# TensorE's loop over the routed expert blocks written out, with fewer loads of expert numbers

## The reference

```
router_probs = softmax(x @ gate_w + gate_b)
values, indices = top_k(router_probs, k=2);  values /= sum(values) + 1e-9
h = gelu(x @ ew1[e] + eb1[e]);  all_outputs[e] = h @ ew2[e] + eb2[e]
moe_out = sum over the two chosen experts of value * all_outputs
return x + mlp_shared(x) + moe_out
```

## Time and profile before

| | |
|---|---|
| median of 3 runs | 920.14 us (920.0 to 920.22) |
| the profiled execution | 923.21 us, span 921.5 us |
| TensorE matmul busy | 686.9 us, 75% of the span |
| VectorE, ScalarE, GpSimd busy | 668.0, 520.6, 474.9 us |
| first routed stage | about 170 to 295 us |
| second routed stage | about 707 to 832 us |

### The profile page before, as it was taken

The page is one execution under the profiler, slowest core; times in us unless marked ns, Lnnn a source line. Parts: engine busy times, 40 slices in busy tenths (PEclk is TensorE's granted clock), DMA queues, the critical chain, the costliest instruction groups (busy, mean ns, idle before and its releaser), DMA issues.

```text
span 921.5 us, 23822 instructions
## 1 busy us (share of the span) xinstructions
PE 686.9 (75%) x7840; PEld 493.2 (54%) x7841; DVE 668.0 (72%) x1374; ACT 520.6 (56%) x1212; POOL 474.9 (52%) x459
## 2 busy tenths in 40 slices
PE   1365299699999258899899899992897999995000
PEld 1243299588889223344344444431896998885000
DVE  7889968477775348899899899967794777772222
ACT  3275454366666144888888888873643766662000
POOL 3974306678780778482340300002256888835775
PEclk9999589799999755999899999996797999998555
DMA  6230210133343111010000000000201233341223
GB/s 181 81 80 0 59 34 1 47 93 84 88 80 55 52 46 35 7 36 14 0 0 0 0 0 0 2 1 23 70 2 30 81 83 90 85 67 49 74 77 86
DMA packets 55995, 43.65 MB, mean 47 GB/s; under 512 B 8228, under 2 KB 50120, under 8 KB 55944
## 3 DMA queue, kind: packets, MB, share of 16 engines
q0 software_dynamic: 9088, 18.63, 9.5%
q1 hardware_dynamic: 46856, 24.35, 9.3%
HBM read 26.44 MB, written 16.52 MB: 47 GB/s over the span
## 4 chain that ended last, share of the span: by engine, by line
PE 47%; POOL 19%; DVE 17%; issue 9%; ACT 3%; DMA 3%; DVEq 1%; SPq 0%; POOLq 0%; ACTq 0%
PE ps L659 26%; POOL scratch L594 10%; POOL gy L608 8%; PE ps L770 6%; PE ps L966 6%; DVE xn L1352 5%; PE ps L785 4%; DVE mx L1656 2%; PE ps L979 2%; DVE hl L1359 1%; PE ps L676 1%; PE ps L824 1%; DMA scratch<-rows,tok_i 1%; DVE rnorm L1380 1%; DMA xres<-in_L_attn_a_x 1%
## 5 line engine op out<-in xcount | busy, mean ns | idle before, releaser
L594 POOL DMA_INDIRECT scratch<-rows,tok_i x156 | 183.2, 1175 | 53.5 <-issue 46.6
L1136 ACT ACTIVATE h<-ps,b1T 128x256 f32<-128x256 f32 x440 | 171.7, 478 | 62.3 <-PE ps L659 62.3
L1656 DVE TENSOR_REDUCE mx<-ps 128x2 f32<-128x512 f32 x256 | 171.3, 687 | 24.9 <-PE ps L659 23.2
L1240 ACT ACTIVATE scratch<-ps 128x512 f32<-128x512 f32 x256 | 148.1, 601 | 36.2 <-PE ps L659 34.7
L608 POOL DMA_INDIRECT gy<-ysorted,slot_i x128 | 122.0, 953 | 76.1 <-DMA ysorted<-yst 38.1
L659 PE MATMUL ps<-xg,w1s 128*128 128x256 f16 x936 | 119.6, 280 | 9.6 <-issue 9.4
L770 PE MATMUL ps<-w2s,hhi 128*128 x1248 | 117.3, 219 | 0.0
L659 PEld LDWEIGHTS ps<-xg,w1s 128*128 x936 | 89.8, 100 | 24.3 <-issue 13.1
L659 PE MATMUL ps<-kst,qst 32*128 32x256 f16 x512 | 93.3, 289 | 8.8 <-DVE mx L1656 8.6
L1505 DVE SCALAR_TENSOR_TENSOR hlo<-h,hhi 128x1024 f16<-128x1024 f32 x78 | 95.6, 1225 | 2.7
L1162 ACT ACTIVATE xg<-ps 128x512 f16<-128x512 f16 x78 | 46.6, 597 | 88.7 <-PE ps L824 88.7
(11 more groups left out here) (215 smaller groups left out, 1348.6 us busy)
## 6 DMA issues: line engine op xcount, KB each, us to landing
ysorted<-yst SPq DMA_DIRECT2D x78, 128.0 KB, 1.8
h<-in_L_ffn_ew SPq DMA_DIRECT2D x16, 256.0 KB, 3.1
rows<-hl SPq DMA_DIRECT2D x8, 512.0 KB, 3.5
scratch<-rows,tok_i POOLq DMA_INDIRECT x156
xres<-in_L_attn_a_x SPq DMA_DIRECT2D x4, 512.0 KB, 5.8
gy<-ysorted,slot_i POOLq DMA_INDIRECT x128, 2.5
out_x<-xres SPq DMA_DIRECT2D x4, 512.0 KB, 3.3
b2s<-in_L_ffn_eb SPq DMA_DIRECT2D x1, 512.0 KB, 4.9
```

Source lines behind the costliest of these rows:

```text
L594: pool.indirect_dma_start(grow[:, BT * (f % 4) + t, :], None, rows_dram[r], bass.IndirectOffsetOnAxis(ap=tok_i[:, n:n + 1], axis=0))\
L1136: last = act.activation(h32[:, u % 2, f], HB[u % 2][:, f], ACT.Gelu_apprx_tanh, bias=b1T[:, ds(e * CH + c, 1)], scale=1.0 / PS)
L1240: act.activation(prb[:, (s // 4 * 4 + (s + 2) % 4) % 8, :], ps[:, s % 2, :], ACT.Exp, scale=HD ** -0.5 / (PS * PS))\
L1656: dve.tensor_reduce(mx[:, c, j:j + 5:4], ps[:, 2 + s % 2, :].rearrange("p (n k) -> p n k", n=2), AX_X, ALU.max).then_inc(Att.mx, 1)
```

## The change

TensorE's hardware loop is replaced by the 39 iterations written out, in the same order of `up_routed`, `turn` and `down_routed`. The numbers of the experts are now loaded when they are first needed and kept in a table `ahead`. At the start 13 elements are loaded (0 to 12), ahead of n = 11 eleven (13 to 23), ahead of n = 22 eleven (24 to 34), and ahead of n = 33 four (35 to 38). That is 4 loads and 39 elements in a stage. Semaphores are compared with constants. Nothing changes on the other engines.

```
-                es = experts(0, 2)
-                up_routed(0, 0, es[0])
+                ahead = {n: e for n, e in enumerate(experts(0, 13))}
+                up_routed(0, 0, ahead[0])
                 turn(2, 2, 0)
-                up_routed(1, 1, es[1])
-                with pe.Fori(0, LOOPED) as i:
-                    es = experts(4 * i, 6)
-                    for u in range(4):
-                        n = 4 * i + u
-                        up_routed(n + 2, (u + 2) % 4, es[u + 2])
-                        turn(n + 3, (u + 3) % 4, i + (u + 3) // 4)
-                        down_routed(n, u, es[u])
-                es = experts(NBLK - 3, 3)
-                for u in range(3):
-                    if u < 1:
-                        up_routed(NBLK - 1, 2, es[2])
+                up_routed(1, 1, ahead[1])
+                for n in range(NBLK):
+                    if n + 2 < NBLK:
+                        if n + 2 not in ahead:
+                            more = experts(n + 2, min(11, NBLK - n - 2))
+                            ahead.update({n + 2 + j: e for j, e in enumerate(more)})
+                        up_routed(n + 2, (n + 2) % 4, ahead[n + 2])
                     else:
-                        up_shared(SA + u - 1)
-                    down_routed(NBLK - 3 + u, u, es[u])
+                        up_shared(SA + n + 2 - NBLK)
+                    if n + 3 < NBLK:
+                        turn(n + 3, (n + 3) % 4, (n + 3) // 4)
+                    down_routed(n, n % 4, ahead[n])
```

## The result

| | before | after |
|---|---|---|
| median of the timed runs | 921.7 us (918.53 to 924.43, 20 runs) | 917.84 us (913.68 to 922.48, 20 runs) |
| ratio | | 0.9958, 95% interval 0.9945 to 0.997 |
| profiled execution | span 921.5 us | span 915.8 us, run 917.55 us |

The change makes the kernel faster by 0.42%, interval 0.3 to 0.55%. On the 921.7 us that is 3.9 us, where 6.3 were forecast. 917.84 lies at the upper end of the range 912 to 918, but the gain is some 60% of the one forecast. Beside the runs of before taken with it the gain is that of rival 1 (920.14 - 916.4 = 3.7 us).

A forecast was written before the change was run, and what follows sets the result against it. TensorE was taken to bound the routed stages. Seams -11.74, loads +5.04 and gathers +0.4 gave -6.3 us, from a median of 920.14 to 913.8 us, range 912.0 to 918.0.

The forecast's parts named there:

- rival 1: Load of eleven from 13: an unaligned start makes all reads singles, 2.6 us more, 916.4 us; chance 0.24.
- The seams: TensorE's lost time between loop passes and at loop exits vanishes: 5.69 us in stage one, 6.05 in stage two, together 11.74.
- the 0.72 at the exit of stage two: Time TensorE lost where stage two leaves its loop, counted among the savings.
- The price of the load of eleven from 13: Load ahead of n = 11: taken as 3 + 2 reads, 0.75 us felt a stage; bound with all singles 2.05.
- head, 13 from 0: Load at a stage's start: three groups and a single, 1.13 us, fully felt, 0.58 over the load of before.
- The 0.57: Microseconds of each inner load expected to lie hidden behind matmuls already handed over, read at the exit of stage one.
- rival 3: Six inner loads: less of each lies hidden behind matmuls, 0.5 us more each, 916.8 us; chance 0.09.
- Instruction supply: Fetches for the longer written-out stream, some 24 to 32 in all, hidden by matmuls: cost 0.
- rival 5: Instruction fetches stop TensorE in the written-out code; at 0.65 us each 18.2 us, 932.0 us; chance 0.05.
- Rival 4: Every element is a read of its own, in long loads at least: slower by 2.8 us, 922.9 us; chance 0.07.
- The gathers: GpSimd's row fetches speed up with TensorE; 0.4 us added for late rows in stage two, between 0 and 1.3.
- Rival 2: Gathers keep their own pace: stage two gains only its exit, 0.72 us, stage one 3.2; 916.2 us; chance 0.09.

The follow-up runs named there:

- c2: Kernel before with its loop kept, but constants as expert numbers and no register loads on TensorE; ratio 1.0018 to the kernel before (922.3 us).
- e2: Kernel before with its loop written out, loads of 12, 12, 12 and 3 from multiples of four; ratios 0.9939 to 0.9966 on 989 us chips, 0.9898 on a 922 us chip.
- c1: Kernel before with its loop written out, constants as expert numbers and no register loads on TensorE; ratio 1.0024 to the kernel before (922.3 us).
- e6: Kernel before with its loop written out, ten loads of four from multiples of four; ratio 0.9919 on a 989 us chip, 0.9888 on a 922 us chip.
- e5: Kernel before with its loop kept, two loads of four from multiples of four in each pass instead of one of six; ratios 0.9945 and 0.9934.
- a1: The changed kernel run again, unaltered, on a 989 us chip; ratio 0.9986 to the kernel before (991.5 us).

## Why the prediction was wrong

**The seams: right.** All of them went, and nothing took their place at other blocks. The mechanism needs one correction. The branch with what surrounds it makes no seam alone (c2: steps of 2.87), and the load would cost little alone (in e2, loads of 0.96 to 1.09 us cost 0.25 to 0.37). It is their sum of 0.57 + 0.82 = 1.4 us that runs over the lead of 0.7 by 0.7. One seam was mis-sized: the 0.72 at the exit of stage two came behind a stop for rows, and in the two later traces of the kernel before that exit loses 0.3.

**The price of the load of eleven from 13: wrong, and this is the step that failed.** The prediction put it at 1.32 us of load and 0.75 felt, "since TensorE's six already mix groups and singles". It took 2.71 and 2.73 us and cost 2.03 and 2.01. The reason given was a reading of the wrong load: the six start at a multiple of four, and so say nothing of a load that doesn't. The one from 13 got no groups at all, though two aligned ones lie inside it. ScalarE's 916 ns for four from 4i + 2 couldn't decide either, since they hold no aligned group, so rival 1 was wrong to count it as support. The rows of before were silent, and the sum took the cheaper of two readings. The dearer adds 2.54 us, about the whole of the missing gain.

**The other terms**, predicted and measured in stages one and two:

| | predicted | measured |
|---|---|---|
| head, 13 from 0 | 0.58 | 0.60, 0.53 |
| n = 11 | 0.75 | 2.03, 2.01 |
| n = 22 | 0.75 | 0.83, 0.82 |
| n = 33 | 0.44 | 0.37, 0.37 |
| sum | 2.52 | 3.83, 3.73 |

Two errors nearly cancel at n = 22 and 33, which is luck: the loads took 1.52 and 1.09 us where 1.32 and 1.01 were expected, and 0.7 us was hidden where 0.57 was expected. The 0.57 was read at the exit of the loop, where more stands ahead of the load than in straight code. So rival 3 (less hidden) is refuted: more is hidden.

With the measured loads the sum is -11.74 + 7.56 = -4.2 us, where the timed runs gave a gain of 3.9 (by the interval 2.8 to 5.1).

**Instruction supply: right.** 55 packets over the span, as forecast (55 to 63), and no stop by "issue" of `up` outside the loads in the stages of the change, and none in those of c1. That refutes rival 5. Rival 4 is refuted by the loads of 12 and 13 elements from an aligned start, which took 0.85 and 1.1 us at their shortest.

**The gathers: a real cost, but not here.** Rival 2 is refuted: stage two gained more than stage one (123.76 - 119.74 = 4.0 us against 2.3, first `up` to last `down_routed`), where only the 0.72 of its exit was left to it. The added 0.4 us had the wrong sign: in the change the stops for rows in stage two were 6.3 us in two, against 6.8 in three before. My reading, which no run isolates, is that the gaps at the long loads give the gathers the time that the seams gave. Where those gaps go too, the cost appears (e6: 1.9 us in stage one). The prediction's "GpSimd has no row of waiting for TensorE" was not quite so: the trace of before has one such wait of 0.3 us.

**Size of the trace's difference.** The two profiled spans differ by 5.7 us, more than the medians. Stage two of the first trace of before was long: 127.09 us from first `turn` to last `down_routed`, against 126.28 and 125.78 in the two later traces. One execution is too few to tell differences of a tenth of a per cent.

## What to carry to other kernels

Count a register load by its reads, not by its elements: start it at a multiple of four elements and take whole groups of four, and widen the tile if the last group needs it. Add up what TensorE's sequencer does between two matmuls, branch and load together, and keep the sum below its lead (0.7 us in this kernel on a 922 us chip). Below it a load alone (e6) or a branch alone (c2) was free. Together they were not, even with a load of 0.33 us (e5, on a 989 us chip). Writing a loop out pays where it parts the two, and no further than the next limit, here the rows. Ten aligned loads of four written out took 0.9888 (0.9861 to 0.9915) and 0.9919 (0.9898 to 0.9939) of the time before, aligned twelves 0.9898 (0.9872 to 0.9924) on another 922 us chip; these runs don't tell which is faster. Nor can the loop with aligned fours be told from either on the 989 us chips (0.9945 and 0.9934).

## What the hardware showed that was not expected

On the 989 us chips the instructions of a block shown here last as long as on the others, the granted clock from 200 to 290 us is 1.00 in both traces, and yet a block takes 3.27 us. The timeline of TensorE's matmul and of ScalarE in the kernel after, first on a 922 us chip, then on a 989 us chip (a1):

```profile
236.05 0.39 PE L824 MATMUL ps<-ident,scratch 128*128 128x128 f16 x4
236.47 0.60 ACT L1159 ACTIVATE xg<-ps 128x512 f16<-128x512 f16 x1 [0.81 <-PE ps L824]
237.61 1.47 PE L659 MATMUL ps<-xg,w1s 128*128 128x256 f16 x12
```
```profile
234.78 0.39 PE L824 MATMUL ps<-ident,scratch 128*128 128x128 f16 x4
...
236.00 0.60 ACT L1159 ACTIVATE xg<-ps 128x512 f16<-128x512 f16 x1 [1.21 <-PE ps L824]
...
236.73 1.48 PE L659 MATMUL ps<-xg,w1s 128*128 128x256 f16 x12 [0.22 <-issue]
```

The transposes end at 236.05 + 0.39 = 236.44 by the record, and ScalarE's copy starts 0.03 us later. On the 989 us chip it starts 236.00 - (234.78 + 0.39) = 0.83 us later, and the next `up` needs the copy. On the 922 us chip that `up` starts 237.61 - (236.47 + 0.60) = 0.54 us after the copy's end, with TensorE busy until then. On the 989 us chip it starts 236.73 - (236.00 + 0.60) = 0.13 us after it, and TensorE stood idle for 0.22. So there the copy seems to hold the `up` back, though the row says "issue". GpSimd, which had hardly waited for TensorE, does so as well. Its waits for it in the first stage, after on a 922 us chip and then a1 (us, times, longest):

```profile
POOL scratch L594 <- PE ps L824: 1.3, 3, 0.7
```
```profile
POOL scratch L594 <- PE ps L824: 30.3, 30, 1.8
```

The ends of matmuls are modelled in a profile, so the records can't say whether the signal or the matmul itself was late, and no run was made to find out. After a long gap, as at the load from 13, TensorE does some blocks in 2.88 us there before it falls back to 3.27, so a gap is partly paid back. That fits the small loss that the change's long load makes on those chips, but it was not tested.
